# Loading VectorE's block index one register at a time, four blocks ahead

## The reference, cut to what matters

```
# 128 blocks; block n has weights W[n] of 64 x 64 channels x 16 taps,
# a source channel block cols[n] and a target channel block rows[n], both drawn at run time (0 to 7)
x_unfold = xb[:, cols]                        # each block reads its source channels
o = conv_general_dilated(x_unfold, W, ...)    # causal, 16 taps
y = zeros.at[:, rows].add(o)                  # and is added to its target channels
```

## Time and profile before

| | us |
|---|---|
| median of the three runs | 873.3 |
| profiled execution, whole time | 872.59 |
| profiled execution, span on the core | 870.8 |
| TensorE busy | 857.7 (98%) |
| VectorE busy | 514.8 (59%) |
| first half addition starts (from the span's start) | 37.20 |
| last half addition starts | 100.81 |

### The profile page before, as it was taken

The page is one execution under the profiler, slowest core; times in us unless marked ns, Lnnn a source line. Parts: engine busy times, 40 slices in busy tenths (PEclk is TensorE's granted clock), DMA queues, the critical chain, the costliest instruction groups (busy, mean ns, idle before and its releaser), DMA issues.

```text
span 870.8 us, 16974 instructions
## 1 busy us (share of the span) xinstructions
PE 857.7 (98%) x5677; PEld 772.4 (89%) x5680; DVE 514.8 (59%) x1342; ACT 431.8 (50%) x1028; POOL 358.7 (41%) x334
## 2 busy tenths in 40 slices
PE   9999899999999999999999999999999999999998
PEld 7999778888888888799989998998997888888887
DVE  4888886333333338887688668768877433333334
ACT  4733425433434344776377557647746433434332
POOL 6754423656556563222121213212112555556552
PEclk9999999999999999999999999999999999999999
DMA  8999321111111102001000100000002111111111
GB/s 337 344 405 402 128 89 40 36 54 46 44 54 36 54 19 75 2 25 38 1 19 6 36 0 24 0 0 1 1 2 73 37 54 46 44 54 36 54 36 49
DMA packets 27859, 61.02 MB, mean 70 GB/s; under 512 B 3554, under 2 KB 11172, under 8 KB 27812
## 3 DMA queue, kind: packets, MB, share of 16 engines
q1 hardware_dynamic: 27812, 60.41, 20.0%
HBM read 59.35 MB, written 1.05 MB: 69 GB/s over the span
## 4 chain that ended last, share of the span: by engine, by line
PE 82%; DVE 10%; ACT 3%; issue 2%; DMA 2%; DVEq 0%; POOL 0%; ACTq 0%
PE bank L1269 29%; PE bank L1793 24%; PE bank L1282 14%; PE bank L1919 4%; DVE cv_acc L549 4%; PE bank L1859 3%; PE bank L1295 2%; PE bank L664 2%; PE bank L1305 2%; DMA cv_shared<-in_wtaps 2%; PE bank L1884 1%; ACT at_prob L1488 1%; DVE stats L74 1%; PE bank L648 1%; DVE xn L100 1%
## 5 line engine op out<-in xcount | busy, mean ns | idle before, releaser
L1168 DVE TENSOR_TENSOR f_h<-f_scaled,bank 128x512 f32<-128x512 f32 (+1 forms) x90 | 60.9, 676 | 179.4 <-POOL f_scaled L1033 166.9
L950 ACT ACTIVATE f_h_hi<-f_h 128x512 fp32r<-128x512 f32 (+2 forms) x102 | 63.6, 624 | 186.6 <-DVE f_h L1168 186.3
L1033 POOL TENSOR_TENSOR f_scaled<-f_act,f_gate_rows 128x512 f32<-128x512 f32 x80 | 103.0, 1288 | 116.1 <-ACT f_act L943 115.8
L1269 PE MATMUL bank<-f_xt_hi,f_w_lo 128*128 128x512 f32 x352 | 138.2, 393 | 0.0
L1269 PE MATMUL bank<-f_xt_hi,f_w_hi 128*128 128x512 f32 x352 | 137.8, 391 | 0.0
L1488 ACT ACTIVATE at_prob<-bank,at_sbias,at_qrs 128x512 f32<-128x512 f32 (+3 forms) x128 | 77.7, 618 | 72.4 <-DVE at_sbias L1680 72.4
L1175 DVE TENSOR_TENSOR f_h_lo<-f_h,f_h_hi 128x512 fp32r<-128x512 f32 (+2 forms) x102 | 71.8, 704 | 70.7 <-ACT f_h_hi L950 70.2
L1269 PE MATMUL bank<-f_xt_lo,f_w_hi 128*128 128x512 f32 x352 | 108.7, 390 | 0.0
L1282 PE MATMUL bank<-f_w_lo,f_h_hi 128*128 128x256 f32 (+1 forms) x352 | 99.6, 283 | 0.0
L1282 PE MATMUL bank<-f_w_hi,f_h_lo 128*128 128x256 f32 (+1 forms) x352 | 99.6, 283 | 0.0
L1282 PE MATMUL bank<-f_w_hi,f_h_hi 128*128 128x256 f32 (+1 forms) x352 | 99.3, 282 | 0.0
(11 more groups left out here) (254 smaller groups left out, 2127.5 us busy)
## 6 DMA issues: line engine op xcount, KB each, us to landing
cv_raw<-in_wconv SPq DMA_DIRECT2D x26, 512.0 KB, 7.6
cv_shared<-in_wtaps SPq DMA_DIRECT2D x32, 384.0 KB, 8.0
f_wraw<-in_w SPq DMA_DIRECT2D x42, 256.0 KB, 2.6
xn<-in_wconv SPq DMA_DIRECT2D x14, 512.0 KB, 7.2
f_wraw<-in_w SPq DMA_DIRECT2D x42, 128.0 KB, 2.5
at_wraw<-in_wqkv SPq DMA_DIRECT2D x3, 768.0 KB, 4.4
at_oraw<-in_wo SPq DMA_DIRECT2D x4, 512.0 KB, 3.5
X<-in_x_tiles SPq DMA_DIRECT2D x2, 512.0 KB, 7.9
```

Of the source, the lines that this page charges most:

```text
L950: a.activation(h_hi[slot][0:rows, cols], h_f[half][0:rows, cols], ACT.Copy).then_inc(s["h_hi_done"], 1)
L1033: g.tensor_tensor(scaled[half][:], act[half][:], gate_rows[:, half * HALF:(half + 1) * HALF], ALU.mult).then_inc(s["scaled_done"], 1)
L1168: v.tensor_tensor(h_f[half][0:rows, cols], src[half][0:rows, cols], pu[half][0:rows, cols], ALU.mult)\
L1269: mm = t.matmul((pg, pu)[gu][half][0:out_rows, :], w, x, start=q == 0, stop=q == 3 * KH - 1)
```

## The change

Each block's register is loaded by an instruction of its own. Four single loads stand ahead of the first block; from there on the register of block i + 4 is loaded between the two half additions of block i. `PB` goes from 8 to 4 and now says how many blocks ahead a load stands. The half additions, their waits and the transfers stay as they are.

```diff
-OB, DB, PB, RING, DRING = 8, 4, 8, 6, 6
+OB, DB, PB, RING, DRING = 8, 4, 4, 6, 6
...
-            def load_pairs(d):
+            def load_pair(i):
                 return nc.values_load_multi_w_load_instructions(
-                    line_pair[0:1, d * PB:(d + 1) * PB], engines=[mybir.EngineType.DVE], min_val=0, max_val=NW - 1,
+                    line_pair[0:1, i:i + 1], engines=[mybir.EngineType.DVE], min_val=0, max_val=NW - 1,
...
             def add_block(i, pairs):
+
+                at = pairs.pop(i)
...
-                    dst = acc[:, :, bass.ds(pairs[i % PB], 1), part].rearrange("p e a f -> p e (a f)")
+                    dst = acc[:, :, bass.ds(at, 1), part].rearrange("p e a f -> p e (a f)")
...
                     add.then_inc(s["added"], 1)
+                    if k == 0 and i + PB < NBLK:
+                        pairs[i + PB] = load_pair(i + PB)
...
-            pairs = load_pairs(0)
+            pairs = {i: load_pair(i) for i in range(PB)}
...
-            for i in range(2, PB):
+            for i in range(2, NBLK):
                 add_block(i, pairs)
-            for p in range(1, NBLK // PB):
-                pairs = load_pairs(p)
-                for i in range(p * PB, (p + 1) * PB):
-                    add_block(i, pairs)
```

More of the change, by code:

```diff
@@ L534, in low_sums @@
                                 row_part(ws_hi[SLOT[f]].bitcast(F32), r), ALU.subtract).then_inc(s["ws_lo_done"], 1)
-            def load_pairs(d):
+            def load_pair(i):
                 return nc.values_load_multi_w_load_instructions(
-                    line_pair[0:1, d * PB:(d + 1) * PB], engines=[mybir.EngineType.DVE], min_val=0, max_val=NW - 1,
-                    skip_runtime_bounds_check_because="columns and rows are numbers of channel blocks, 0 to 7 each")[1]
+                    line_pair[0:1, i:i + 1], engines=[mybir.EngineType.DVE], min_val=0, max_val=NW - 1,
+                    skip_runtime_bounds_check_because="columns and rows are numbers of channel blocks, 0 to 7 each")[1][0]
             def add_block(i, pairs):
+                at = pairs.pop(i)
                 d, n = divmod(i, DB)
```

## The result

The changed kernel takes 890.71 us (median of four runs, 890.61 to 890.86) beside 872.89 for the kernel before (median of four). It is 17.8 us slower. The ratio on record is 1.0195, with a 95% interval of 1.0172 to 1.0218 (the two medians alone divide to 1.0204). The prediction had the sign and the mechanism, and said 40 us.

What follows compares the result with a forecast made beforehand. VectorE's half additions were taken to bound the first phase and so the end: -8.2 + 1.5 + 54.6 - 2.0 - 4.6 - 0.9 = +40 us on 872.6 gives 913 us, range 875 to 932.

Steps and rivals of the forecast that it cites:

- What sets the end: First phase: VectorE's last half addition sets the kernel's end; it starts near 141 us and everything behind moves as a block.
- A load holds the queue: VectorE's queue: a load holds everything behind it, even what needs no register, so loading four blocks ahead hides nothing.
- My sign for it: Test in VectorE's profile after: no address computation and no half addition starts between a load's start and end.
- A load hides 0.05 us: VectorE's loop: each load hides only 0.05 us behind half additions, so a block takes L + 0.29 us, L the load's length.
- The length of a load of one, 0.49 us: VectorE's 124 loop loads: each takes 0.49 us, from TensorE's only single load, adding 54.6 us.
- a later start of 0.8 us and not 1.5: VectorE ahead of the first block: three more loads in a row, +1.5 us.
- my rival of a short load: VectorE's single load takes 0.12 to 0.38 us; at 0.25, +11 us, 884 us; chance 0.24.
- The allowance that I had set aside for the lower case: TensorE's first load: taking off 0.245 us, VectorE's first-load excess, from 0.49 gives 0.25 us.
- How the waits are taken up: VectorE's additions: loads take up 2.0 us of block waits, 4.6 of slower additions, 0.9 of two long ones.
- The price of one against eight: VectorE's load of one lies between 0.60 us (count costs nothing) and 0.075 us (an eighth of the load of eight).
- TensorE is done early and idles: First phase: TensorE's sums come late but finish before VectorE's additions; only its clock costs, at most 2 us more.
- The delay is passed on in full, a gain hardly: End of the first phase: VectorE's delay moves the end fully; without load cost TensorE bounds the gain, 870 us.

Runs made afterwards that it cites:

- Experiment 10: The changed kernel with the transfers for TensorE's sums further ahead of VectorE's in SyncE's queue: 890.77 us, 1.0197 times the kernel before.
- experiment 1: The changed kernel with each single register loaded right ahead of its own block, not four blocks ahead: 891.3 us, 1.0192 times the kernel before.
- experiment 2: The kernel before with its fifteen later loads of eight registers each moved four blocks ahead of first use: 873.29 us, 1.0009 times.
- experiment 11: The changed kernel with two single loads to a block, one behind every half addition: 937.47 us in one run.
- experiment 4: The kernel before with unused loads ahead of the first block; VectorE's were not in the program, TensorE's two extra were: 874.21 us in one run.
- experiment 5: The kernel before with thirteen groups of 1 to 32 blocks, one load each, in place of sixteen groups of eight: 893.59 us in one run.
- experiment 9: The kernel before with loads of many sizes, most starting at multiples of four words: 886.04 us in one run.
- experiment 3: The kernel before without its fifteen loads between groups, so sums land in wrong rows: 873.82 us, 0.9989 times.
- experiment 6: The changed kernel with two registers to a load, at every other block, four blocks ahead: 890.04 us, 1.0193 times the kernel before.
- experiment 7: The changed kernel with four registers to a load, four blocks ahead: 874.1 us, 1.0016 times the kernel before.
- experiment 8: The kernel before with its table of pairs starting one word (4 bytes) later in SBUF: 886.82 us, 1.0154 times.

## Why the prediction was wrong, step by step

- **What sets the end: right.** The time moved by 17.8 us, the last half addition by 17.9, and what stands behind it not at all. Experiment 10 excludes TensorE from it.
- **A load holds the queue: right.** Read from one row of the first load, shown by experiments 1, 2 and 11 and by the address computations, none of which starts inside a load in any run. My sign for it was too strict: half additions do start inside loads, since one handed over before the load begins some 0.02 us after it. By that sentence as it stands I would have been wrong; the address computations are the test.
- **A load hides 0.05 us: right.** The block's pitch was to be L + 0.29 us; with L = 0.301 that is 0.59, measured 0.59.
- **The length of a load of one, 0.49 us: wrong, and the step that failed.** It is the term 124 x (0.49 - 0.05) = 54.6 us, which with the measured 0.301 is 124 x (0.301 - 0.05) = 31.1 us. That is the whole difference between the 40 us forecast and the 17.8 measured, and a little more: 40.4 - 23.5 for this term, - 0.7 for a later start of 0.8 us and not 1.5, + 1.7 for the waits below, is 17.9. What came was my rival of a short load (0.12 to 0.38 us), to which I had given 0.24; its own point, 884 us for a load of 0.25, was 7 us too low. I took TensorE's single load because it was the nearest row, though the same trace showed what a first load costs more (0.245 us on VectorE). The allowance that I had set aside for the lower case was the better reading: TensorE's second load takes 0.312 us (experiment 4). With 0.30 in the sum: 31.0 - 8.2, 0.8 for the later start, and "about 6" taken up, as I had written for the short load, gives 17.6 us, or 890.2. That this comes so near is in part luck, for the 6 was a rough number; with the 7.5 of the forecast it would be 888.7.
- **How the waits are taken up: right in kind, too large.** I took off 2.0 + 4.6 + 0.9 = 7.5 us. Measured is the remainder 31.1 - 8.2 + 0.8 - 17.9 = 5.8 us. The transfers' 3.0 us of waits are gone, as I had said; so the slower and the long additions took up 3.8 us, not 5.5.
- **The price of one against eight.** Both of my ends assumed one law for all counts (all fixed, or all by the count), and I had a chance only for values between. The law has steps and depends on the start. The Trainium skill's rule of some 0.2 us for each register (Runtime: NRT & Kernel Launch, Instruction fetch mechanics) I called refuted by the eight in 0.60 us. That page speaks of loads from HBM; for words from SBUF that aren't read by fours the runs show 0.22 each, which is near it. The floor of 0.6 us (DMA: Bandwidth & Descriptors, Latency and other measured facts) doesn't hold for these loads: 0.30 and 0.34 us lie below it.
- **TensorE is done early and idles: wrong.** It idled 2.03 us for one late transfer, ran at the lower clock for 34 us, and ended 0.33 us before VectorE. I had priced its clock at 2 us at most, behind the additions, where it cost nothing (770.0 us on both sides); ahead of them it took up all the room there was. It is luck that this didn't make the kernel slower still: in experiments 5 and 9 the same thing costs 5 and 10 us.
- **The delay is passed on in full, a gain hardly: right**, more so than said: the gain from no loads is none (experiment 3), not 3 us.

## What to carry to other kernels

A register load holds its engine's queue for all of its length, so loading earlier doesn't hide it. Load fewer times and in whole fours of words, and check in the profile that the table starts where a load reads four words at once: here loads from multiples of four words of the table did, and four bytes of shift lost it. Before a single unusual row is used as a price, correct it for what the trace shows of first executions. Price a removed stall by what is late next, and an added one also by what it holds back in a shared transfer queue: a wait of 1.0 to 2.8 us for a late transfer put TensorE on its lower clock for 27 to 44 us in five of the kernels here and in the changed kernel.

## What the runs showed of the hardware

- A load of n registers from SBUF, as an estimate from the lengths of experiments 5 to 9: 0.09 us, 0.25 for each four words if it starts at a multiple of four words of this table, 0.22 for each other word; 0.18 to 0.26 us more for an engine's first load. A table moved by 4 bytes made the kernel 1.54% slower (experiment 8).
- After idling 1.0 to 2.8 us in the middle of dense work TensorE was granted 0.50 of its clock for 27 us (experiments 8 and 9), 31 us (experiment 1), 34 us (changed kernel and experiment 6) and 44 us (experiment 5), though in the changed kernel it was busy 33.4 of 34 us. In experiment 10, without that idling, it kept its full clock until it ran out of work. Not every such wait does it: in experiment 2 it idled 0.97 us ahead of 89.93 us, in experiment 11 1.42 us ahead of 61.89 us, and both times the clock held, as the timeline and the stretches of experiment 11 show. It fell there at 68.11 us, inside a wait of 3.64 us, and stayed at 0.50 until 143.2 us. What ends such a stretch stays open: in the changed kernel the clock came back at 115.02 us with no wait of TensorE just before it.

```profile
61.89 2.00 PE L664 MATMUL bank<-cv_onehot,xn 128*128 128x64 f32 x16 [1.42 <-DMA xn<-in_wconv]
68.99 3.67 PE L664 MATMUL bank<-cv_onehot,cv_raw 128*128 128x64 f32 x16 [3.64 <-DMA cv_raw<-in_wconv]
...
61.90:68.10 6.20, 3.46 (x28) 3.25 (x28) 3.81 (x13) 0.83 (x3) 0.91 (x2) 1.00 0.59 201
68.10:143.20 75.10, 63.77 (x292) 62.64 (x293) 42.74 (x152) 12.54 (x43) 11.85 (x21) 0.50 0.59 192
```

- GpSimd's subtraction of 128 x 128 took 4.95 us in place of 0.46 while VectorE's additions ran without a gap (experiment 3), and two others 5.68 and 5.02. By the Trainium skill (SBUF — State Buffer, Terms) the two engines share a port pair that one holds exclusively and the other waits for. The trace agrees in part. Each of the three ends within 0.4 us of a gap in VectorE's additions, and GpSimd's operation of 2.4 us at 87.96 us stretched the addition beside it to the same 2.4 us. But the 4.95 us span 27 additions in a row, not one, and a subtraction of 0.46 us got through in the same unbroken run.
